# Attention on one core: the blocks for a group's maxima run 16 ahead instead of 8, the shifts are made two steps early, and the rings of PSUM banks run on over groups

## The reference, cut to what matters

```python
x = x + 0.5 * _L0_ffn_ref(_layernorm(x), ...)
x = x + _L0_attn_ref(_layernorm(x), Wq, bq, Wk, bk, Wv, bv, Wo, bo)
x = x + 0.5 * _L0_ffn_ref(_layernorm(x), ...)
...
q = (x @ Wq + bq).reshape(b, s, HQ, DH).transpose(0, 2, 1, 3)
k = x @ Wk + bk
v = x @ Wv + bv
scores = jnp.einsum('bhsd,btd->bhst', q, k) / scale
attn = jax.nn.softmax(scores, axis=-1)
out = jnp.einsum('bhst,btd->bhsd', attn, v)
out = out.transpose(0, 2, 1, 3).reshape(b, s, HQ * DH)
return out @ Wo + bo
```

## Time and profile before

| what | value |
|---|---|
| median of 3 runs | 3214.35 us |
| lowest, highest | 3210.79, 3216.09 us |
| the profiled execution, first to last instruction | 3211.7 us |
| of it the attention stage, by the profile's clock | about 817 to 2541 us |

### The profile page before, as it was taken

The page is one execution under the profiler, slowest core; times in us unless marked ns, Lnnn a source line. Parts: engine busy times, 40 slices in busy tenths (PEclk is TensorE's granted clock), DMA queues, the critical chain, the costliest instruction groups (busy, mean ns, idle before and its releaser), DMA issues. The chain is left out here.

```text
span 3211.7 us, 44845 instructions
## 1 busy us (share of the span) xinstructions
PE 2799.2 (87%) x15264; PEld 1631.1 (51%) x15264; DVE 2037.6 (63%) x3922; ACT 1526.7 (48%) x2871; POOL 2216.7 (69%) x1430
## 2 busy tenths in 40 slices
PE   8967777398899999999999999999999876888870
PEld 4644444176555555555555555555554374555540
DVE  7833222267788788788787887887876294333334
ACT  5522222153566566566565665665656352222220
POOL 2248888562688788788787887887878423677770
PEclk9978888699999999999999999999999867999995
DMA  5679999894567677676776776776757364899998
GB/s 213 214 203 241 246 235 235 198 276 168 118 146 145 132 171 146 147 148 140 154 150 132 172 142 147 147 145 149 155 121 153 104 212 154 202 233 234 243 184 321
DMA packets 216987, 575.78 MB, mean 179 GB/s; under 512 B 33980, under 2 KB 35004, under 8 KB 192824
## 3 DMA queue, kind: packets, MB, share of 16 engines
q0 software_dynamic: 87296, 343.98, 53.2%
q1 hardware_dynamic: 125240, 220.55, 21.1%
q10 hardware_dynamic: 4224, 8.39, 0.7%
HBM read 230.94 MB, written 155.24 MB: 120 GB/s over the span
## 5 line engine op out<-in xcount | busy, mean ns | idle before, releaser
L1915 DVE TENSOR_REDUCE attention_mx<-attention_pM 128x1 f32<-128x512 f32 x1984 | 1209.4, 682 | 180.1 <-PE attention_pM L1774 175.7
L1719 ACT ACTIVATE attention_prob<-attention_pS 128x512 f32<-128x512 f32 x2048 | 1035.9, 628 | 528.7 <-PE attention_pS L1761 528.5
L1660 POOL TENSOR_TENSOR attention_pair<-attention_prob 128x1024 f32<-128x1024 f32 x380 | 947.4, 2499 | 189.4 <-ACT attention_prob L1719 174.7
L1761 PE MATMUL attention_pS<-attention_qT,prep_kT 128*128 128x512 f32 x2048 | 832.7, 413 | 2.5 <-ACT attention_prob L1719 1.5
L1774 PE MATMUL attention_pM<-prep_kT,attention_qT 96*128 96x512 f32 x1984 | 804.4, 408 | 0.0
L1761 PEld LDWEIGHTS attention_pS<-attention_qT,prep_kT 128*128 128x128 f32 x2048 | 387.3, 189 | 289.4 <-issue 160.0
L1799 PE MATMUL attention_pO<-attention_prob,attention_v 128*32 128x512 f32 x4096 | 492.5, 598 | 0.0
L768 POOL DMA_INDIRECT sum<-experts_res,c_table x256 | 404.0, 1578 | 123.2 <-issue 78.0
L1774 PEld LDWEIGHTS attention_pM<-prep_kT,attention_qT 96*128 96x128 f32 x1984 | 374.7, 190 | 142.2 <-DVE attention_mx L1915 56.8
L752 POOL DMA_INDIRECT experts_rows<-xn_rows,c_table x256 | 250.7, 979 | 103.8 <-issue 71.3
L797 PE MATMUL experts_pT<-c_ident,experts_rows 128*128 128x128 f32 x1024 | 169.5, 306 | 120.2 <-issue 47.9
(11 more groups left out here) (181 smaller groups left out, 3141.3 us busy)
## 6 DMA issues: line engine op xcount, KB each, us to landing
prep_acc<-attention_pair POOLq DMA_DIRECT2D x96, 1024.0 KB, 7.7
attention_acc<-attention_pair POOLq DMA_DIRECT2D x90, 1024.0 KB, 7.6
attention_qT<-q_parts SPq DMA_DIRECT2D x96, 256.0 KB
xn_rows<-route_xn SPq DMA_DIRECT2D x16, 1152.0 KB, 6.7
experts_wup<-in_L_ffn_w_up_dram SPq DMA_DIRECT2D x64, 256.0 KB
q_parts<-prep_acc SPq DMA_DIRECT2D x64, 256.0 KB, 4.3
ahead_wup<-in_L_ffn_w_up_dram SPq DMA_DIRECT2D x64, 256.0 KB, 9.1
combine_got<-sum SPq DMA_DIRECT2D x16, 1024.0 KB
```

Of the source, the lines that this page charges most:

```text
L1660: pool.tensor_tensor(to[:, part], prob[2 * n % PROBS][:, part], prob[(2 * n + 1) % PROBS][:, part], ALU.add).then_inc(s_pair, 1)
L1719: act.activation(prob[t % PROBS][:, h * QT:(h + 1) * QT], pS[:, at, :], ACT.Exp).then_inc(s_ex, 1)
L1761: pe.matmul(pS[:, at, :], kT[:, key:key + P], qT[g][:, h, :], start=True, stop=True).then_inc(s_sc, 1)
L1915: dve.tensor_reduce(mx[:, unit, part:part + 1], pM[:, r % RING, :], X, ALU.max).then_inc(s_mr, 1)
```

## The change

A group is written as 8 equal phases. Phase `p` holds the scores of steps 2p and 2p+1 with 8 blocks between them, then, where there are any, the transposes of the next group's shifts (`COPY_PAIR`, phase 6), an output tile, the denominators of the group before (`SUM_PAIR`, phase 4), and last the values of the two steps before, which in phase 0 are the last two of the group before. Phases 0 to 5 hold the last 48 blocks of group G+1, phases 6 and 7 the first 16 of group G+2. The first group, which has no phases before it, takes all 64 blocks of group 1 in phases 0 to 5 (11, 11, 11, 11, 10, 10) and 8 in each of the last two; the last two phases of group 30 and all of group 31 have none. DVE makes the shifts at the end of phase 5 and copies its two heads in phase 6, before the reciprocals; ACT copies its two after step 13. The negated maxima go to an SBUF tile `whole` instead of a bank of `pM`. The rings of 3 and 4 banks are counted over the whole stage (`at_bank`, `freed`, `bank_free`), with the transposed shifts as an item of the ring. The wait for the output weights moves from the start of PE's stream to the first output tile.

```diff
-        EARLY = 2
-        AT_HEAD = (0, 0, 1, 1, 1, 1, 1, 1)
-        AT_PAIR = (8, 8, 8, 8, 8, 8, 8, 0)
-        OUT_PAIRS = (1, 2, 4, 6)
-
-        SUM_PAIR = 3
-        RECIPROCAL_PAIR = 5
...
+        AHEAD = 2 * HG * 2
+        FIRST_BLOCKS = (11, 11, 11, 11, 10, 10)
+        OUT_PAIRS = (2, 3, 5, 7)
+        SUM_PAIR = 4
+        SHIFT_PAIR = 5
+        COPY_PAIR = 6
+        RECIPROCAL_PAIR = 6
...
+        def blocks_in(G, k):
+
+            if k >= SHIFT_PAIR + 1:
+                n = 2 * HG * (k - SHIFT_PAIR - 1)
+                return [(G + 2, n + i) for i in range(2 * HG)] if G + 2 < GROUPS else []
+            if G + 1 >= GROUPS:
+                return []
+            n = sum(FIRST_BLOCKS[:k]) if G == 0 else AHEAD + 2 * HG * k
+            return [(G + 1, n + i) for i in range(FIRST_BLOCKS[k] if G == 0 else 2 * HG)]
...
+                        if t == 2 * COPY_PAIR + 1 and G + 1 < GROUPS:
+                            for h in (2, 3):
+                                copy_shift(G + 1, (G + 1) % GPC, h)
...
+                def bank_free(r):
+
+                    old = r - RING
+                    if old in shift_of:
+                        pe.wait_ge(s_sha, A + (shift_of[old] + 1) * 2)
+                        pe.wait_ge(s_shd, A + (shift_of[old] + 1) * 2)
+                    elif old >= 0:
+                        pe.wait_ge(s_mr, A + freed[old])
...
+                def phase(G, p):
+
+                    r = at_bank[G, p]
+                    blocks = blocks_in(G, p)
+                    for i in range(2 * HG):
+                        scores(G, 2 * p + i // HG, i % HG)
+                        for of, n in blocks[len(blocks) * i // (2 * HG):len(blocks) * (i + 1) // (2 * HG)]:
+                            maxima(r, of, n)
+                            r += 1
+                    if p == COPY_PAIR and G + 1 < GROUPS:
+                        transposed_shifts(r, G + 1)
+                        r += 1
+                    if output_in(G, p) is not None:
+                        output(r, G // GPC - 1, output_in(G, p))
+                        r += 1
+                    if p == SUM_PAIR and G > 0:
+                        denominators(r, G - 1)
+                    for t in (2 * p - 2, 2 * p - 1):
+                        if p > 0:
+                            values(G, t)
+                        elif G > 0:
+                            values(G - 1, STEPS + t)
...
-                    whole = pM[:, 1, 0:UNITS]
-                    dve.tensor_reduce(whole, mx[:, :, :], X, ALU.max, negate=True).then_inc(s_mx, 1)
+                    dve.tensor_reduce(whole[:, :], mx[:, :, :], X, ALU.max, negate=True).then_inc(s_mx, 1)
...
+                def phase(G, p):
+
+                    r, count = at_bank[G, p], at_count[G, p]
+                    for _, n in blocks_in(G, p):
+                        maxima(r, count, n)
+                        r, count = r + 1, count + 1
+                    if p == 0 and G > 0:
+                        copy_o(*divmod(G - 1, GPC))
+                    if p == SHIFT_PAIR and G + 1 < GROUPS:
+                        make_shifts(G + 1, count)
+                    if p == COPY_PAIR and G + 1 < GROUPS:
+                        for h in range(2):
+                            copy_shift(G + 1, (G + 1) % GPC, h)
+                        r += 1
+                    if output_in(G, p) is not None:
+                        output(r, count, G // GPC - 1, output_in(G, p))
+                        r, count = r + 1, count + 1
+                    if p == SUM_PAIR and G > 0:
+                        copy_d(r, count, G - 1)
+                    if p == RECIPROCAL_PAIR and G > 0:
+                        reciprocals(G - 1)
```

More of the change, by code:

```diff
@@ new lines, in output_in, with count_items @@
+        def output_in(G, k):
+            return OUT_PAIRS.index(k) if G % GPC == 1 and G > GPC and k in OUT_PAIRS else None
+        at_bank, at_count, freed, shift_at, outputs_done = {}, {}, [], {}, {}
+        def count_items():
+            count = 0
+            for G in range(GROUPS):
+                for k in range(PAIRS):
+                    at_bank[G, k], at_count[G, k] = len(freed), count
+                    for _ in blocks_in(G, k):
+                        count += 1
+                        freed.append(count)
+                    if k == COPY_PAIR and G + 1 < GROUPS:
+                        shift_at[G + 1] = len(freed)
+                        freed.append(None)
+                    if output_in(G, k) is not None:
+                        count += 1
+                        freed.append(count)
+                        outputs_done[G // GPC - 1] = count
+                    if k == SUM_PAIR and G > 0:
+                        count += 1
+                        freed.append(count)
+            return count
@@ L1879, in group @@
+                pe.wait_ge(s_init, 1)
+                transposed_shifts(0, 0)
+                for G in range(GROUPS):
+                    for p in range(PAIRS):
+                        phase(G, p)
+                        if G == GROUPS - 1:
                             for q in LAST_SUMS[p]:
                                 last_sums(q)
-                    if not last:
-                        if not (static and c == CHUNKS - 1 and nxt == GPC - 1):
-                            end = static and c == CHUNKS // 2 - 1 and nxt == GPC - 1
-                            early(c + 1 if nxt == 0 else c, nxt, 1 if end else ahead)
-                        scores(G + 1, nxt, 0, 0, ahead)
@@ L1887, in body @@
-                def body(c, batch):
-                    for g in range(GPC):
-                        group(c, g, batch)
-                pe.wait_ge(s_init, 1)
-                transposed_shifts(0)
-                early(0, 0, 0)
-                scores(0, 0, 0, 0, 0)
-                pe.wait_ge(s_wo, A + 16)
-                chunks(body)(pe)
+                for t in (STEPS - 2, STEPS - 1):
+                    values(GROUPS - 1, t)
+                last_sums(5)
                 last_sums(6)
@@ L1996, in _ @@
                     copy_shift(0, 0, h)
-                chunks(body)(dve)
+                for G in range(GROUPS):
+                    for p in range(PAIRS):
+                        phase(G, p)
                 dve.wait_ge(s_lsum, A + PAIRS)
```

201 lines of the change are left out of this document (58 added, 143 removed).

## The result

The changed kernel ("after" below) takes 3285.95 us (3279.63 to 3292.08) where the kernel before takes 3214.99: a ratio of 1.0225, with an interval of 1.021 to 1.0241. It is 71 us slower; the forecast was 35 us faster. The profiled execution of after has a span of 3290.4 us, 78.7 above that of before. I work with spans from here on, since the stages and groups are read from them.

A forecast was written before the change was run, and what follows sets the result against it. PE itself was taken to bound ordinary phases, with gaps at group boundaries. Savings of 35.3 us (24 plain boundaries) and 6.7 (7 after output tiles), less 6.8 for group 0, gave 35.2 us: 3179 us, range 3168 to 3194.

The forecast's parts named there:

- (1): Group boundary: with shifts ready early, two ordinary intervals of 5.78 replace gaps of 13.70 us, saving 2.14 us.
- (2): Transposes moved to phase 6 behind a block: PE's path grows by 0.59 us, bounds 0.51 to 1.1.
- (3): Denominators behind the blocks: same matmuls, plus a wait for a bank of 0.08 us, between 0 and 0.60.
- (4): DVE's shifts, copies and reciprocals fit the holes between phases: cost nothing, 0.44 us of slack covering 0.15 of lateness.
- (6): The 7 boundaries after output tiles: no gap left to save, the head is the same; 0.96 us saved each.
- (7): Group 0 makes 16 more blocks, costing 7.8 us; the output weights' wait of 0.98 goes, net 6.8 us lost.
- the first rival: DVE's late phase 6 copies make phases 7 and 0 wait for banks, 0.8 us per group: 3204 us, chance 0.12.
- the second: Rival: another engine, POOL, has the period, so it stays at 50.17 us and nothing is gained: 3214 us, chance 0.06.
- part (5): ACT's 8 exponentials and two copies fit in a phase at no cost; SP's order unchanged, its DMAs' reciprocals left to rivals.
- the third rival: Later reciprocals delay POOL's normalising multiply, stopping ACT, then PE; landing 4 us later loses 2.4 per group: 3251 us, chance 0.06.

The follow-up runs named there:

- the kernel with the reciprocals first: The changed kernel with DVE's reciprocals ahead of its two shift copies in phase 6, nothing else changed: 3180.21 us, ratio to before 0.9894.
- the run with the fault in the kernel before: The kernel before, with DVE's reciprocals moved behind one more block, about 1.6 us later: 3254.09 us, ratio to before 1.0114.
- the last experiment: The changed kernel with reciprocals behind the fifth of phase 6's eight blocks and POOL's multiply one pair later: 3176.3 us, ratio to before 0.9876.
- the runs with 32 KB: The changed kernel in its own order, with the accumulating DMA of pair 5 moving 64 of 2048 columns: 3180.68 us, one run.
- with the reciprocals between the copies: The changed kernel with DVE's reciprocals between the two shift copies of phase 6: 3186.9 us, ratio to before 0.9919.

## Why the prediction was wrong

**What held.** Steps (1) to (4), (6) and (7) came out to a few tenths, as the kernel with the reciprocals first shows, which has all of them. A plain period is 48.62 there (48.70 was forecast), shorter than before by 1.54 where 1.47 was forecast; one with output tiles is 63.17 against 64.30, so 1.13 where I had 0.96; the transposes cost 6.36 - 5.79 = 0.57 for 0.59; group 0 lost 6.35 for 6.8. PE's last matmul of the stage starts at 2505.4, where it was 2540.5: 35.1 us earlier, 35.2 forecast. That is closer than the parts are, and so it is partly luck: the groups with output tiles gave 7.9 us for 6.7, and the stage's first score came 1.1 later (820.98 for 819.88). The time of that kernel, 3180, is the 3179 of the forecast. No first score of groups 1 to 31 waits, and the first rival (DVE's carry-over) did not come: phase 7 is 5.79 there, and 5.87 in after. Nor did the second: with POOL's work unchanged, taking gaps from PE's path brought 1.06%. By the rule of the Trainium skill, Perfetto Trace Analysis, Identifying the Most-Contended Engine, POOL would have come first; the measurement decides against that here.

**What failed** is one step, in part (5) and in the third rival. Part (5) says that SP's order isn't changed, but the reciprocals on which its DMAs wait are, and sends the reader to the rival. There I put the reciprocals 7.1 us into phase 6, which they are (43.59 after the group's first score, with phase 6 beginning at 36.5), and then added 9.5 us from reciprocals to multiply, a duration read in the old place, as if it belonged to the operation. It belonged to the place: the write-back in it had a start of 0.34 us on a transfer of a megabyte. In the new place it is 13.8 us at the least, so the multiply comes not 4.5 but 8.7 us or more into the next group. The growth of 4.3 is that of the write-back's landing, 5.9 for 1.7. I read DVE's, POOL's and ACT's rows but not SP's beside POOL's DMA issues, where the 0.34 us stand.

My reason against this rival, that the old 9.5 is bounded by POOL and not by the landing, was a wrong reading too. In the trace of before the last of the four spreading DMAs lands 0.17 us ahead of the multiply's start in 22 of 30 groups (971.15 and 971.32 at the end of group 2), and 0.26 to 0.30 ahead in the others; in after, where POOL stands waiting for that landing, it is the same 0.17, and 0.26 in seven. POOL's sum before it ended at about the same time, which hid that the landing had next to no slack: what the landing lost, the multiply lost.

**The rival's mechanism and price.** It was named in the prediction, with its chain, and given 0.06. Its margin was nearly right: multiplies at 5.1 to 5.9 us into the group cost nothing, and the three groups whose clock stayed at 1.00 lost 2.8, 2.5 and 2.8 us to multiplies at 9.11, 9.00 and 9.14, which is 6.3 to 6.5 if each us late costs one, where the prediction has 6.1. By its price, what the 22 late multiplies lie beyond 6.1 sums to 75.0 us; 3176.5 + 75.0 is a span of 3251.5. That this is near the rival's 3251 is luck: it had 2.4 us in each of 30 groups, and here it is 2.6 to 4.7 in 22. Measured is 3290.4. The missing term is the clock: behind the waits PE works for some microseconds at half its rate, which adds up to 3.0 us in a group. Group 11 has the latest multiply: it comes at 10.76, 4.66 beyond, and phase 2 loses 7.36. Phase 2's 112.4 less 75.0 leaves 37.4 for the clock. That is a remainder, but the groups bear it out one by one: the three with a granted clock of 1.00 leave nothing (-0.2 to -0.4), the nine with 0.97 or 0.98 leave 1.2 to 1.4, and the ten with 0.94 or 0.95 leave 2.3 to 3.0.

## What to carry to other kernels

When an instruction moves, every transfer that it releases moves too: set its new issue time beside the issues of the large transfers on the other queues, and don't carry its old landing time along. A small transfer on a chain of several (load, write back, spread) belongs ahead of a large one, or its consumer belongs behind work that others wait for; either remedy alone gave back 3.2%. Where a rival has PE wait inside a busy stretch, its price has to allow for a slower clock behind the wait, which came here in 19 of 22 groups. And two events that come out together, as the landing and POOL's free moment did here, are no proof that one of them has slack.

## What the runs showed of the hardware

An 8 KB transfer to DRAM from SP's queue, issued 1.23 us behind the start of an accumulating 1 MB transfer's issue on POOL's queue, landed after 5.9 to 7.7 us, where 0.3 us ahead or 0.5 us behind it landed in 1.4 to 1.7 in most groups. It waits the large one out: in each of those 29 groups of after it landed 0.16 to 0.78 us behind the large one's own landing. So it did in the run with the fault in the kernel before, issued 1.27 to 2.88 behind, and in most groups of the last experiment, at 3.66 + 3.45 = 7.1 from the start of the large one's issue.

The DMA records of the traces, which the views above don't list one by one, show what waits. The large transfer moves in 128 pieces of 8 KB, the first of which begins 1.42 to 1.49 us after the start of its issue in all groups of after; the small one has 128 pieces of 64 B, which begin 0.83 after their issue where no large piece stands ahead (in the runs with 32 KB and with the reciprocals between the copies). In after they begin at 4.0 to 4.6, and half of them only at 5.3, when 127 or all of the 128 large pieces have begun. So the data themselves stand behind the large one's, and not only the signal that they have landed. An estimate from these figures: the small one is ahead if it is issued less than 1.43 - 0.83 = 0.60 us behind the large one, which lies between the 0.50 and the 1.23 that were run.

The Trainium skill, DMA: Bandwidth & Descriptors, section Queues, rings and completion order, says that each DMA engine goes round the queues and drains a whole packet, typically some 9 to 17 descriptors, of one before it turns to the next. This fits the records: the large one's 128 pieces and 16 writes of 4 bytes are nine for each of 16 engines, which may be one packet; no run here tells whether they are. The same section says that the semaphore's write lands only after every earlier write of that engine, across its queues; that isn't what held the small one up here, since its data began late.

PE's waits alone don't tell when the clock falls. In group 3 it was 1.00 up to a second wait, of 1.95 us some 3 us behind one of 1.50, and fell to 0.50 behind it. In group 24 it fell in a single wait, of 1.93, and was 0.94 over the group; in group 4 waits of 0.26 and 1.94 left it at 1.00.
